# Two half steps of the second hop moved to the head of the first relation pass

## The reference, cut to what matters

```python
# layer 3: two hops over the edges, then a dense product
for _ in range(2):
    msg = segment_sum(norm[:, None] * h[src], dst, N)
    h = 0.5 * msg + 0.5 * x
x = x + relu(h) @ W.T + b
# layer 4: two relation layers (8 relations, 256 x 256 weights each)
xt  = einsum('ni,rio->rno', x, W)          # every node times every relation's weights
msg = relu(xt[edge_type, src] + b)         # gathered by edge
h   = segment_sum(msg, dst, N)             # done twice, with W0 and W1
```

## Time and profile before

| what | value |
|---|---|
| median of 3 runs | 2688.56 us (2685.17 to 2694.28) |
| the profiled execution's own time | 2689.72 us |
| its span, first to last instruction | 2687.9 us |
| PE / DVE / ACT / POOL busy | 2387.7 / 1336.4 / 572.3 / 1620.1 us |
| `rel1a` on PE | from 1507.6 us (first half step) to 1890.1 us |
| `rel1b` on PE | first visit at 1901.6 us |
| last gather issued | 2675.1 us |

### The profile page before, as it was taken

How to read it: one execution, slowest core, us unless ns; L and a number is a source line. 1 busy time by engine, 2 the same in 40 slices (tenths; PEclk the granted TensorE clock), 3 DMA queues, 4 the chain that set the end, 5 groups by cost and what they waited for, 6 DMA issues and landing times.

```text
span 2687.9 us, 41486 instructions
## 1 busy us (share of the span) xinstructions
PE 2387.7 (89%) x11183; PEld 1798.7 (67%) x11184; DVE 1336.4 (50%) x2819; ACT 572.3 (21%) x1718; POOL 1620.1 (60%) x1701
## 2 busy tenths in 40 slices
PE   7799999999699999999999799998799798766666
PEld 4589999999456588888777477775455555544444
DVE  6788888888676721112373334443344334322232
ACT  1366666666000000000111101111122022000000
POOL 5777777720057777777100377664675757777776
PEclk9899999999799999999999999999899899887887
DMA  3033333322366688553443456653565455333443
GB/s 111 22 118 112 115 115 115 115 114 113 117 191 188 185 315 277 159 180 110 165 148 115 159 161 193 183 159 95 166 184 159 128 154 179 109 103 104 121 120 102
DMA packets 203201, 388.37 MB, mean 144 GB/s; under 512 B 52864, under 2 KB 136942, under 8 KB 202890
## 3 DMA queue, kind: packets, MB, share of 16 engines
q1 hardware_dynamic: 52356, 180.31, 20.0%
q0 software_dynamic: 66944, 111.48, 15.7%
q10 hardware_dynamic: 83718, 94.32, 10.3%
HBM read 244.89 MB, written 141.08 MB: 144 GB/s over the span
## 4 chain that ended last, share of the span: by engine, by line
PE 71%; DVE 10%; issue 8%; POOL 5%; DVEq 2%; ACT 2%; DMA 1%; PEldq 0%; SPq 0%; POOLq 0%; PEld 0%; ACTq 0%
PE agg L1045 16%; PE agg L1166 14%; PE y L922 13%; PE agg L986 9%; PE y L963 5%; POOL gathered L819 5%; PE y L1045 4%; PE agg L1041 4%; PE prod L907 2%; PE y L966 1%; DMA gathered<-table_rel,idx_rel 1%; ACT gathered L1295 1%; DVE onehot L1983 1%; PE y L865 1%; PE turn_ps L892 1%
## 5 line engine op out<-in xcount | busy, mean ns | idle before, releaser
L819 POOL DMA_INDIRECT gathered<-table_rel,idx_rel x840 | 809.4, 964 | 580.4 <-ACTq L1411 258.2
L1166 PE MATMUL agg<-gathered,onehot 128*128 x2072 | 577.3, 435 | 192.4 <-DVE onehot L1983 113.6
L1166 PEld LDWEIGHTS agg<-gathered,onehot 128*128 128x128 f32 x2072 | 434.6, 218 | 328.5 <-issue 262.8
L1983 DVE SCALAR_TENSOR_TENSOR onehot<-iota,keybase,edges 128x256 f32<-128x256 f32 x518 | 240.9, 484 | 642.7 <-PE agg L1166 542.5
L803 POOL DMA_INDIRECT edges_parted<-stream x416 | 402.3, 967 | 179.9 <-issue 126.5
L764 POOL DMA_INDIRECT edges_bucketed<-edges,stream x416 | 401.4, 965 | 148.7 <-issue 122.6
L986 PE MATMUL agg<-h_sb,stream 128*128 128x257 f32 x1250 | 334.9, 392 | 0.0
L1045 PE MATMUL agg<-gathered,stream 128*128 128x256 f32 x1250 | 271.7, 381 | 0.0
L1045 PEld LDWEIGHTS agg<-gathered,stream 128*128 128x128 f32 x1250 | 239.2, 191 | 32.6
L963 PE MATMUL y<-gathered,rel_sb 128*128 128x128 f32 x1300 | 234.8, 290 | 12.6 <-ACT gathered L1295 11.2
L963 PEld LDWEIGHTS y<-gathered,rel_sb 128*128 128x128 f32 x1300 | 218.2, 192 | 36.2 <-ACT gathered L1295 14.4
(11 more groups left out here) (209 smaller groups left out, 2405.3 us busy)
## 6 DMA issues: line engine op xcount, KB each, us to landing
table_rel<-rel_sb ACTq DMA_DIRECT2D x200, 256.0 KB, 3.1
stream<-weights_dense SPq DMA_DIRECT2D x41, 832.0 KB
stream<-weights_dense SPq DMA_DIRECT2D x41, 768.0 KB
weights_dense<-stream SPq DMA_DIRECT2D x25, 832.0 KB, 3.4
stream<-counts_dense SPq DMA_DIRECT2D x50, 416.0 KB
table_rel<-zeros ACTq DMA_DIRECT2D x16, 1280.0 KB
weights_dense<-stream SPq DMA_DIRECT2D x25, 768.0 KB, 3.2
stream<-counts_dense SPq DMA_DIRECT2D x50, 384.0 KB
```

Of the source, the lines that this page charges most:

```text
L819: pool.indirect_dma_start(gathered[:, slot * D:(slot + 1) * D], None, tables[n], bass.IndirectOffsetOnAxis(ap=idx_rel[:, c:c + 1], axis=0) ...
L1166: mm = pe.matmul(agg[b][:, 0:D], onehot[:, place * 2 + k, :], gathered[:, bass.ds(((p + pairs0) & (GP - 1)) * (2 * D) + k * D, D)], start= ...
L1983: nc.vector.scalar_tensor_tensor(onehot[:, place * 2:place * 2 + 2, :], iota[:].unsqueeze(1).broadcast_to([P, 2, P]), keybase[:, bass.ds(t ...
```

## The change

`step_at` gives way to `steps_with(t)`: tile 0 of `rel1a` gets the half steps 0, 1 and 2, and tile t from 1 on the half step t + 2. Tile 22 then has h = 24; tiles 23 and 24 have h = 25 and 26, in which no engine has anything to do. The same on PE and on DVE. ACT's and SP's code is as before.

```diff
-        def step_at(i):
-
-            return STEPS[(i + 1) // 2], (i + 1) % 2
+        def steps_with(t):
+
+
+            halves = range(3) if t == 0 else (t + 2,)
+            return [(EARLY + h // 2, h % 2) for h in halves]
...
+            def hop2_steps(t):
+                for s, half_ in steps_with(t):
+                    hop2_step(s, half_)
+
...
-                     "rel1a": [(-1, lambda t, b: hop2_step(*step_at(t - 1)), range(TILES))],
+                     "rel1a": [(-1, lambda t, b: hop2_steps(t), range(TILES))],
...
-                               (lambda: hop2_step(*step_at(t - 1))) if n == "rel1a" else None)
+                               (lambda: hop2_steps(t)) if n == "rel1a" else None)
...
+            def hop2_steps(t):
+                for s, half_ in steps_with(t):
+                    hop2_step(s, half_)
```

## The result

The changed kernel takes 2664.16 us (median of 5 runs, 2661.32 to 2670.82), the kernel before 2685.17 us beside it (median of 5, 2681.72 to 2694.28). The ratio is 0.9919, with a 95% interval of 0.9905 to 0.9934: about 22 us faster. The profiled execution took 2663.22 us, with a span of 2661.4 us. The two profiled executions are 26.5 us apart; 2.9 us of that lie ahead of the pass, where both kernels run the same code, and are chance.

The account below looks back on a forecast made before the run. The end was taken as POOL's last full-ring stop plus fixed gathers, moving with PE's first `rel1b` visits. Gain 17.4 + 1.3 = 18.7, say 19 us; 2688.56 - 19 = 2669.6 us, 8-in-10 range 2660.5 to 2679.5.

Parts of the forecast that it names:

- Who bounds what: After the seam, the end moves as much as PE's first visits of `rel1b`, not as much as POOL's restart.
- POOL's ring stop ahead of the seam: In tile 20 of `rel1a`, POOL's last full-ring stop, ended at 1838.20 before, moves by 1 or 2 us.
- its gap: POOL's wait for ACT between the last early and first late gather shrinks from 33 to about 5 us.
- its restart: POOL's first late gather, at the seam, comes 27.3 us earlier, at 1863.7 instead of 1890.97.
- The rival in which POOL's restart decides: At the seam, gathers alone hold `rel1b`'s early visits, so the whole 27.3 us go through: 2661 us; chance 0.14.
- The start: Head of `rel1a`: two added half steps cost PE 2.9 us; its wait for gathers hides the other ten.
- my term of 29.3 us: From tile 1's end to tile 15's relation products, 29.3 us as before, so these start at 1577.0, 27.3 us earlier.
- The block load: At the start, ACT's load of tile 16's blocks, issued at 1513.46, taken as landed by 1520.8; bound 1522.9.
- The end of the pass: Tiles 22 to 24 behind the last products at 1851.7: `rel1b`'s first visit at 1884.2 against 1901.59, gain 17.4 us.
- The first rival: Tiles 23, 24 and `rel1b`'s first three lose the clock: gain 10 to 13 us, 2676 to 2679; chance 0.22.
- The slower rival: Clock stays low in `rel1b`'s first products: two such tiles cancel the gain, four give 2714 us; chance 0.04.
- After the seam: Rest of the kernel untouched: `rel1b`'s products shift with PE, and POOL's last stops shift by the same.

Follow-up runs that it names:

- two traces of before: Profiles of the unchanged kernel before: the first one, and a repeat on another chip that took 2688.97 us (one run).
- the release put off: Changed kernel plus 48 waited-for copies on ACT ahead of the late quads' release: ratio 0.9995 to the kernel before, at 4060 us.
- neither half alone: Against the kernel before at 4060 us: early half steps at the start only, 1.0018, 1.0001, 0.9997; moved from tile 12 on only, 0.9999, 0.9978, 0.9996.
- two first: Half steps 0 and 1 with tile 0, then t + 1, instead of the changed kernel's three: 0.9917 of the kernel before, at 4060 us.

## Why the prediction was right, and where its terms were off

The forecast was 2669.6 us with 2660.5 to 2679.5 around it; measured were 2664.16. Of the 5.4 us between, 3.4 are the kernel before, whose median moved from 2688.56 to 2685.17 with two more runs. The gain was 19 us by the sum and 21 to 22 us by the runs.

**Who bounds what** held. POOL's ring stop ahead of the seam moved by 1.6 us (1 or 2 forecast), its gap fell to 5.36 us (about 5), its restart moved by 29 us, and the end by 22. The rival in which POOL's restart decides asked for all of it. The two traces of before and the one after settle this at 2685 us: the place of the layer-2 products moved by 20, POOL's first long ring stop by 18.9 to 22.0. The direct test of it, the release put off, was made at 4060 us and settled nothing.

**The start** was sized at 2.9 us for two half steps and cost 0.4 us at the end of tile 1. Two terms were too large. The visits were counted at 1.13 us each, the length of one that stands alone; in a run of five they take 4.48 us, 0.90 each. And the visits of tile 0 ended at 1529.90, which is 1.1 us earlier than the sum had it (1533.9 less the 2.9 us between the traces), with no restart of 0.5 us behind them. Five of the six visits of tile 1 were so done before the last pair landed. The sum also counted only idle time as what pays for the move, and left out that a PE that idles less ran these visits at a clock of 1.00 instead of 0.91. PE then waits 2.27 us for the rows of the next turn, which my term of 29.3 us for the two following tiles held already: measured 66.8 - 37.6 = 29.2. That gives the last products 29.6 us earlier instead of 27.3. The block load, of which I had only a bound, was in time.

**The end of the pass** was sized at 32.5 us from the last products to `rel1b`'s first visit and took 1879.20 - 1846.45 = 32.75. The terms shifted among each other: tile 22 took 13.5 instead of 14.5, tile 23 9.4 as sized, tile 24 7.0 instead of 6.0.

**The first rival was partly true.** It gave the bare tiles a lower clock, and 1856 to 1886 shows 0.83. Six visits of tile 23 took 7.47 us, where six in the middle of the pass take 5.7. It did not cost the gain, since my visits were sized too long by about the same, and since before PE's idleness at the seam slowed the same first visits of `rel1b` (6.98 us, now 6.27; I had 5.65). The advice of the Trainium skill, "TensorE: Matmul & The Clock Gate", section "Why this matters for your kernels", which concerns only longer gaps, was not enough here: the clock fell with gaps of 1.88 to 2.93 us between visits. The slower rival asked for a clock still low in the layer-2 products, and that stretch is at 1.00.

**After the seam** I let the shift pass through unchanged. The 48 products ahead of `rel2a` took 1.7 us less, 20.87 us instead of 22.49 and 22.56, at a granted clock of 1.00 instead of 0.93 and 0.92. By POOL's long ring stop the shift was 22.0 us against the first trace of before, 2 us more than at the layer-2 products, and 18.9 us against the second, 1 us less. So I count nothing here for the change: the last gather alone differs by 4.4 us between the two traces of before.

**That both parts are needed** is what the decomposition suggests and what I can't prove at 2685 us. There `rel1a` as a whole, on PE, before and after, is

```profile
1507.55:1890.11 382.56, 347.91 (x1348) 254.74 (x1348) 140.44 (x316) 36.18 (x71) 246.72 (x256) 0.96 0.51 156
```

```profile
1504.66:1876.27 371.61, 344.45 (x1348) 252.38 (x1348) 140.46 (x316) 36.18 (x71) 259.04 (x270) 0.98 0.55 171
```

so half of the 20 us is in this pass: 7.5 us less idle and 3.5 us less busy time for the same 1348 matmuls. The rest is the seam (11.5 us of waiting to 2.9). At 4060 us neither half alone gave a gain that held, and the changed kernel gave 13 us.

## What to carry to other kernels

When a transfer engine waits for a product that stands last in a pass, moving it forward is worth what the engine that fills or empties the ring behind it gains, not the wait itself: here 33 us of waiting became 5, and 22 came through. Look for the idle time that pays for the move, at the head of the same pass in this case, and cost it by the row of the wait that it fills. Count a series of instructions by the length of the series, not by that of one that stands alone.

## What the runs showed that I had not expected

The same program took 2685 us on some chips and 4060 to 4077 us on others, with gathers and one-hots of equal length and with single waits of up to 35 us on PE and DVE that no engine of this core ends. Whether the chip or something else makes the pace is open. The waits repeat with the order of the work. At that pace the 22 us of the change shrank to 13, and an order of half steps that my sum had no reason to prefer (two first) was timed at 34 us. A gain of less than 1% that comes from the order of the work should be timed at the pace at which it was predicted.
